# Later offsets for the side jobs that follow an attention in a four-layer attention and FFN kernel

## What is computed

```python
x = x + attn_a(layernorm(x))      # q, k, v, o projections, softmax over the past
x = x + ffn(layernorm(x))         # r = sigmoid(xr W_r); k = relu(xk W_k)^2; r * (k W_v)
x = x + attn_b(layernorm(x))      # k: decayed sum, normed, scaled; v: mixed with the next token's, normed
x = x + ffn(layernorm(x))
```

## Time and profile before

| | |
|---|---|
| median of 3 runs | 3308.53 us (3307.43 to 3314.87) |
| profiled execution, its own time | 3312.66 us |
| span of the trace in it | 3310.9 us |
| TensorE busy | 2950.6 us, 89% |
| ScalarE busy | 2226.6 us, 67% |
| VectorE busy | 1442.7 us, 44% |
| GpSimd busy | 830.9 us, 25% |
| mean granted TensorE clock | 0.944 of full speed |

### The profile page before, as it was taken

The page is one execution under the profiler, slowest core; times in us unless marked ns, Lnnn a source line. Parts: engine busy times, 40 slices in busy tenths (PEclk is TensorE's granted clock), DMA queues, the critical chain, the costliest instruction groups (busy, mean ns, idle before and its releaser), DMA issues.

```text
span 3310.9 us, 99622 instructions
## 1 busy us (share of the span) xinstructions
PE 2950.6 (89%) x42980; PEld 1307.6 (39%) x42980; DVE 1442.7 (44%) x3534; ACT 2226.6 (67%) x2487; POOL 830.9 (25%) x1278
## 2 busy tenths in 40 slices
PE   7799999999998799997998999998999988999887
PEld 3333343333434244443444444433333333333343
DVE  5232245545544652434333333444555545522444
ACT  2588876777776377673776677776777764777562
POOL 4122223233322222221222221322333321312111
PEclk9899999999999799997999999999999998999898
DMA  5222212222221123222222223221222221222111
GB/s 139 82 81 74 85 43 71 71 70 71 70 59 46 53 61 95 69 61 66 82 65 67 84 76 90 61 63 50 71 71 69 71 55 34 70 66 79 44 44 49
DMA packets 229841, 225.66 MB, mean 68 GB/s; under 512 B 33221, under 2 KB 212933, under 8 KB 229320
## 3 DMA queue, kind: packets, MB, share of 16 engines
q1 hardware_dynamic: 228504, 217.47, 23.0%
q10 hardware_dynamic: 816, 0.79, 0.1%
HBM read 146.80 MB, written 71.32 MB: 66 GB/s over the span
## 4 chain that ended last, share of the span: by engine, by line
PE 68%; DVE 17%; issue 8%; ACT 5%; POOL 1%; SPq 1%; DMA 1%; DVEq 0%; ACTq 0%; POOLq 0%
PE ps L857 42%; PE ps L1064 22%; ACT probs L813 4%; PE ps L869 3%; DVE pmax L1366 2%; DVE ln_st L1138 2%; DVE xn L1147 2%; DVE nw_u L1128 1%; DVE nw_u L1130 1%; DVE nw_y L1132 1%; DVE k_blk L1345 1%; DVE x_buf L1259 1%; DVE ln_mv L1141 1%; DVE o_blk L1408 1%; POOL probs L716 1%
## 5 line engine op out<-in xcount | busy, mean ns | idle before, releaser
L813 ACT ACTIVATE probs<-ps 128x1024 f32<-128x1024 f32 x2176 | 2078.0, 1093 | 714.5 <-PE ps L857 711.2
L857 PE MATMUL ps<-q_st,k_st 99*32 99x512 bf16 (+3 forms) x20480 | 1275.1, 353 | 43.2 <-issue 26.1
L1064 PE MATMUL ps<-probs,v_st 128*17 128x512 f32 (+3 forms) x10240 | 1201.0, 541 | 111.3 <-issue 76.5
L857 PEld LDWEIGHTS ps<-q_st,k_st 99*32 99x32 bf16 x20480 | 565.7, 97 | 850.8 <-issue 460.2
L716 POOL TENSOR_SCALAR_AFFINE_SELECT probs<-probs 128x256 f32<-128x256 f32 (+1 forms) x896 | 405.3, 468 | 1533.3 <-ACT probs L813 1526.5
L1064 PEld LDWEIGHTS ps<-probs,v_st 128*17 128x17 f32 x10240 | 288.7, 99 | 390.3 <-issue 169.5
L1408 DVE STREAM_TRANSPOSE o_blk<-ps 128x512 f32<-128x512 f32 x128 | 90.7, 709 | 449.6 <-PE ps L1064 447.7
L857 PE MATMUL ps<-xT,wT 128*32 128x512 f32 x2048 | 251.5, 609 | 1.8 <-issue 1.8
L869 PE MATMUL ps<-ident,xn 128*128 128x128 f32 x512 | 97.3, 323 | 117.6 <-DVE o_blk L1408 59.2
L1259 DVE TENSOR_TENSOR x_buf<-x_buf,ps 128x512 f32<-128x512 f32 x64 | 43.7, 683 | 316.9 <-PE ps L857 313.1
L640 POOL TENSOR_TENSOR parts<-rest,parts 128x512 bf16<-128x512 f32 x96 | 119.7, 1247 | 226.1 <-DVE parts L1170 226.1
(11 more groups left out here) (136 smaller groups left out, 2170.1 us busy)
## 6 DMA issues: line engine op xcount, KB each, us to landing
part_a<-parts SPq DMA_DIRECT2D x192, 128.0 KB
x_buf<-in_L_attn_a_X SPq DMA_DIRECT2D x32, 512.0 KB, 4.6
q_st<-part_a SPq DMA_DIRECT2D x128, 128.0 KB
o_chan<-o_out SPq DMA_DIRECT2D x64, 256.0 KB, 2.4
o_in<-o_chan SPq DMA_DIRECT2D x64, 256.0 KB, 4.5
q_st<-part_b SPq DMA_DIRECT2D x128, 128.0 KB
k_st<-part_a SPq DMA_DIRECT2D x64, 192.0 KB, 2.9
part_b<-parts SPq DMA_DIRECT2D x96, 128.0 KB
```

The lines of the kernel that those rows point to most:

```text
L813: nc.scalar.activation(probs[:, g % NP_BUF, :], ps[:, bk:bk + 2, :].rearrange("p a n -> p (a n)"), ACT.Exp, scale=SCALE[ATT[g // (NHG * NG ...
L857: last = pe.matmul(o[c:c + 32], kt[:, c:c + 32], q, **how)
L1064: last = pe.matmul(ps[32 * j:32 * j + VW, bank, q0:q0 + w], v_st[:, k % 2, kb, hg * HG + j, :], p, start=(kb == 0), stop=(kb >= TB * qc), ...
```

## The change

No instruction of the computation is added or removed; tables of offsets change, and with them the places at which parts stand. In the FFN half (`T_M`) the turns, `diff` and `shift` move back by 4 slots, `k0`, `k1`, `r0`, `r1` too, and `f0`, `f1`, `out` by 3. In the B half (`T_B`) `bt0` to `bv1` move back by 6 slots, `w` and `u` by 5, `vt0`, `vt1`, `len` and `split` by 4, `vb` by 2, `low` and `store` by 1; the layernorm before it (`lnb`) is numbered 3 later. The MB jobs of instances 28 to 31 keep the old offsets in a new table `T_END`; P jobs keep theirs. So that tables can differ from job to job, each job holds its own (`off`), and all steps read it there.

```diff
+    def __init__(self, kind, b, c, att, t0, off=None):
+        self.off = off or OFFSETS[kind]
...
-T_M = {"load": -10, "o0": 0, "o1": 2, "t0": 9, "t1": 11, "diff": 11, "shift": 13, "k0": 16, "k1": 18, "r0": 20,
-       "r1": 22, "f0": 25, "f1": 27, "out": 30}
-T_B = {"bt0": 34, "bt1": 36, "bk0": 38, "bk1": 40, "bv0": 42, "bv1": 44, "w": 46, "u": 48, "vt0": 51, "vt1": 53,
-       "len": 56, "split": 58, "vb": 64, "low": 67, "store": 71}
+T_M = {"load": -10, "o0": 0, "o1": 2, "t0": 13, "t1": 15, "diff": 15, "shift": 17, "k0": 20, "k1": 22, "r0": 24,
+       "r1": 26, "f0": 28, "f1": 30, "out": 33}
+T_B = {"bt0": 40, "bt1": 42, "bk0": 44, "bk1": 46, "bv0": 48, "bv1": 50, "w": 51, "u": 53, "vt0": 55, "vt1": 57,
+       "len": 60, "split": 62, "vb": 66, "low": 68, "store": 72}
+T_END = {"load": -10, "o0": 0, "o1": 2, "t0": 9, "t1": 11, "diff": 11, "shift": 13, "k0": 16, "k1": 18, "r0": 20,
+         "r1": 22, "f0": 25, "f1": 27, "out": 30}
...
-    jobs += [Job("MB", 2, c, 7, start(7, c) + FRONT if c < 3 else start(7, 2) + 32) for c in range(NCH)]
+    jobs += [Job("MB", 2, c, 7, start(7, c) + FRONT if c < 3 else start(7, 2) + 32, T_END) for c in range(NCH)]
...
-                  for name, off in {"P": (("ln", 0),), "MA": (("ln", 2), ("lnb", 27)), "MB": (("ln", 2),)}[j.kind])
+                  for name, off in {"P": (("ln", 0),), "MA": (("ln", 2), ("lnb", 30)), "MB": (("ln", 2),)}[j.kind])
...
-                yield j.t0 + T_M["diff"]
+                yield j.t0 + j.off["diff"]
```

More of the change, by code:

```diff
@@ L139, in job_list @@
             jobs.append(Job("P", b + 2, c, k + 1, start(k, c) + 29))
-    jobs += [Job("MB", 2, c, 7, start(7, c) + FRONT if c < 3 else start(7, 2) + 32) for c in range(NCH)]
-    jobs += [Job("MB", 3, c, 7, start(7, 3) + (16, 37, 58, 82)[c]) for c in range(NCH)]
+    jobs += [Job("MB", 2, c, 7, start(7, c) + FRONT if c < 3 else start(7, 2) + 32, T_END) for c in range(NCH)]
+    jobs += [Job("MB", 3, c, 7, start(7, 3) + (16, 37, 58, 82)[c], T_END) for c in range(NCH)]
     jobs.sort(key=lambda j: j.t0)
@@ L176, in number_parts @@
 def number_parts():
-    order = sorted((j.t0 + OFFSETS[j.kind][name], i, seq, name)
+    order = sorted((j.t0 + j.off[name], i, seq, name)
                    for i, j in enumerate(JOBS) for seq, name in enumerate(PE_PARTS[j.kind])
@@ L440, in m_job @@
             def m_job(j):
-                yield j.t0 + T_M["load"]
+                yield j.t0 + j.off["load"]
                 load_x(j)
                 load_o(j)
-                yield j.t0 + T_M["out"]
+                yield j.t0 + j.off["out"]
                 n = j.at["job"]
@@ L546, in _ @@
                     j = JOB["P" if ATT[k][0] == "A" else "MA", ATT[k][1], c]
-                    there = FIRST_SLOT if hg else j.t0 + (T_P["u3"] + T_P["store"] if j.kind == "P" else T_B["store"] + 2) + 2
+                    there = FIRST_SLOT if hg else j.t0 + (j.off["u3"] + j.off["store"] if j.kind == "P" else j.off["store"] + 2) + 2
                     loads.setdefault(max(free[0], there), []).append((load_queries, n, c))
@@ L644, in p_job @@
                 if j.c == 0:
-                    yield j.t0 + T_P["u0"]
+                    yield j.t0 + j.off["u0"]
                     if j.att >= 2:
@@ L700, in m_job @@
                 for m in range(KT):
-                    yield j.t0 + T_B["low"] + 2 * m
+                    yield j.t0 + j.off["low"] + 2 * m
                     low_part(j.at["unit"] + m)
@@ L914, in p_job @@
                         last.then_inc(s_part, 1)
-                if at == T_P["flag"] and j.c == NCH - 1:
+                if at == j.off["flag"] and j.c == NCH - 1:
                     part = j.at["flag"]
@@ L924, in m_job @@
                 for i in range(2):
-                    if at == T_M[f"o{i}"]:
+                    if at == j.off[f"o{i}"]:
                         if f == 0:
@@ L1263, in m_job @@
                 for kt in range(KT):
-                    yield j.t0 + T_M[f"t{kt}"]
+                    yield j.t0 + j.off[f"t{kt}"]
                     copy_out(j.at[f"t{kt}"], xf[:, kt, 1:CH + 1])
-                yield j.t0 + T_M["shift"]
+                yield j.t0 + j.off["shift"]
                 for buf, w, done in ((buf_k, 1, s_xk), (buf_a, 0, s_xr)):
@@ L1346, in m_job @@
                 settle()
-                yield j.t0 + T_B["split"]
+                yield j.t0 + j.off["split"]
                 for m in range(KT):
```

75 lines of the change are left out of this document (37 added, 38 removed).

## The result

| | before | after |
|---|---|---|
| median | 3310.93 us (4 runs beside those of after) | 3283.76 us (3280.78 to 3284.98) |
| ratio | 1 | 0.9916, 95% interval 0.9899 to 0.9933 |
| profiled execution's own time | 3312.66 us | 3280.78 us |
| span of its trace | 3310.9 us | 3279.1 us |
| mean granted clock | 0.944 | 0.958 |

The change makes the kernel faster by 27 us in the medians and by 31.8 us in the profiled executions, by their spans. Forecast were 44 us, a median of 3265 us, with 3225 to 3302 us as the range.

A forecast was written before the change was run, and what follows sets the result against it. TensorE, busy 89% of the span, sets the pace; its 360 us idle and lower-clock time can change. Terms -132 + 19 - 25 + 20 + 46 + 21 + 7 = -44 us gave 3265 us, range 3225 to 3302.

The forecast's parts named there:

- First turns, -132: Slots 5 to 12, 24 jobs: 8.6 us instead of 14.1, one 1.9 us wait left in slot 6; -132 us.
- Clock behind slot 6, +7: 24 jobs: a clock fall after the 1.9 us wait in slot 6, taken as 0.3 us a job; +7 us.
- the rival in which every job loses by it, and half of the gain with it: Slot 6's wait lowers the clock in every job; 53 us come back instead of 7; about 3310 us; chance 0.11.
- Masks behind `diff`, +19: Slot 14, 24 jobs: products wait 0.8 us for a GpSimd mask, bounds 0 and 1.5; +19 us.
- The rival that had the masks hidden: Clock stays up and masks are hidden, so +19, +21, +7 fall away; -91 us, 3218 us; chance 0.12.
- `bt0`, -25: Slot 30, 16 MA jobs: `bt0`'s 1.57 us wait for the layernorm goes; -25 us.
- slot 40, +20: 16 MA jobs: with `bt1` in slot 38, segment 3's first products wait 0.89 or 1.61 us; +20 us.
- End of an MA job, +46: 16 MA job ends: VectorE finishes later and `o1` starts 2.9 us later, bounds 2.2 and 3.5; +46 us.
- its clock, +21: 16 MA job ends: lower clock after TensorE's idle time makes `o1` cost 1.3 us more; +21 us.
- The clock rule that spoke against the change: A loop where TensorE waits each round is throttled each time; at `o1` every end pays 1.7 us, 27 instead of 21.
- All else, 0: Parts moved as blocks, the shorter `bv1` to `vt0` gap, SP loads and stores, ScalarE's exponentials: counted at nothing.

The follow-up runs named there:

- take_first: diff_apart with VectorE's layernorm behind `o1` placed behind the take of segment 3 instead of ahead of it; 3236.43 us, 0.9772.
- diff_apart: The changed kernel with the second token difference on GpSimd two slots behind the first; 3266.72 us, 0.9867.
- bt_early: The changed kernel with `bt0` and `bt1` alone two slots earlier, in slots 34 and 36; 3266.75 us, 0.9858.
- keys_apart: shift_two with key and value parts in turn (`bv0` in slot 38, `bk1` in 40, `bv1` in 42); 3189.68 us, 0.9642.
- shift_two: Against the kernel before: FFN-half steps and `bt0` to `bk0` two slots later, `bk1` one, everything from `bv0` on as before; 3212.27 us, 0.9700.
- low_behind: combo with `low` at 74 and `store` at 78, behind the masks of the next instance's first groups; 3236.57 us, 0.9767.
- combo: keys_apart with the split at 69, `vb` 66, `low` 70, `store` 74; 3215.48 us, 0.9713.

## Why the prediction was right, and where it was off

- **First turns, -132.** Right in mechanism: no wait ahead of the turns, one wait in slot 6, its releaser the take in 22 of 24 jobs. The stretch takes 9.05 us in MA jobs against 8.6 worked out, so 5.0 a job instead of 5.5. It counted the wait as the 1.9 us of a take that can't come earlier; take_first shows that it can.
- **Clock behind slot 6, +7.** Three stretches at clock 0.84 to 0.85 (instances 4, 19, 20) take 6 us more than the usual 8.9 in all, of which about 5 are the clock and the rest the longer wait. The size is right, and the rival in which every job loses by it, and half of the gain with it, is refuted. But this was luck. The forecast had a wait of 1.9 us and took the clock to stay up behind it; the wait came out at 1.1 to 1.7 us in twenty jobs. Over all fourteen kernels, where slot 6 held the only wait of its stretch, the clock fell behind 14 of 16 waits of 1.92 to 2.15 us. With a wait of the length forecast in every job, the rival could well have come true.
- **Masks behind `diff`, +19.** This is the term that was mis-sized: +39.6, 1.65 a job, over my upper bound of 1.5. The step that failed is the single wait of 0.8 us in slot 14. I let GpSimd catch up behind it. It does not: three of its six masks take 0.85 us beside VectorE's mixing, not 0.41, and to a wait of 0.49 us in slot 14 comes a second of 0.87 in slot 16. (The two make 1.36 us; the stretch grows by some 0.14 more for each, in diff_apart too.) At 0.41 us each the masks would be out 1.3 us earlier, which is more than 0.87, so by this estimate the second wait is the price of the overlap. The rival that had the masks hidden is refuted.
- **`bt0`, -25, and slot 40, +20.** -24.8 and +23.1. The waits of turns for a layernorm went from 54.0 us in 19 to 29.9 in 3; bt_early removes the wait of slot 40 alone.
- **End of an MA job, +46, and its clock, +21.** Over the twelve ends of instances 4 to 9 and 20 to 25 `o1` starts on average 2.87 us later than before (forecast 2.9) and takes 3.31 instead of 2.03 us, 1.28 more (forecast 1.3). Still the sixteen ends cost 59.9 us and not 67. Twelve (all but those of instances 8, 9, 10 and 26) cost 4.1 to 5.9, 57 us in all and 4.8 each where 4.2 were forecast: `o1` starts 3.0 us later there, takes 1.5 more, and 0.3 lie behind it. Instances 8 and 9, where `o1` was late before as well, cost 1.5 and 2.4, and 10 and 26, where slot 64 alone takes some 40 us, nothing. I had multiplied by 16 what holds for 12.
- **The clock rule that spoke against the change.** At `o1` the traces agree with the Trainium skill ("TensorE: Matmul & The Clock Gate", section "HAM oscillation — how this bites in real kernels"): eleven of the first twelve ends have an `o1` of 3.1 us or more, against 1.91 at the higher level. In slot 6, where TensorE also waits for data in every job, they don't: 1.00 in 21 of 24 stretches. The loop on that page waits longer, though, some 3 to 5 us.
- **All else, 0.** It is -8.9 us, of which -4 lie in slots 54 to 63 of MA jobs and some -4 at ends of instances without an MA job; I tested neither.

The sum is nearer than its terms. The turns, masks and slot 40 came out 28 us worse than forecast, the ends and all else 16 us better, and these cancel in part by luck.

What stays open: no run moved VectorE's mixing away from the masks. That they stretch by it rests on the comparison of masks with and without it in the same trace.

## What to carry to other kernels

When side work is moved later in an interleaved order, move it no further than the wait needs: two slots back (71 us under after) took the wait at the turns and left the last engine's work where it was. Ask of every bank what stands ahead of its release in the releasing engine's own order; here one `yield` that puts a take ahead of a layernorm was worth 30 us, and putting 5 us of work ahead of a release lost 26. When a wait for several semaphores names one releaser, check its time against all others: the mask named in slot 1 had ended 1.0 us before, and the kernel built on it was to gain 15 us or more over keys_apart and lost 47. Before a step of GpSimd is moved, look at what VectorE runs in its new place: `low` beside the layernorm cost more than `low` beside the split.

## What the runs showed of the hardware

- The granted clock of slots 5 to 11, where slot 6 held the only wait over 0.15 us from slot 67 on, over the traces of all fourteen kernels: behind 37 waits of 0.92 to 1.53 us it stayed at 1.00 each time, behind 68 of 1.70 to 1.73 it fell once (shift_two, instance 23, 0.84), behind 16 of 1.92 to 2.15 it fell 14 times, to 0.84 or 0.85, and behind 6 of 3.13 to 4.09, all in low_behind, each time. Behind the wait of 3.89 us ahead of `o1` it was 0.50, and `o1` took 3.81 us against 1.91.
- On GpSimd a mask of 128 x 256 takes 0.40 to 0.41 us with VectorE idle (348 in after) and 0.85 to 0.86 where it runs beside VectorE's step of line 1273 with two SBUF inputs (49 in after); one of 128 x 512 takes 0.63 us and 1.08 (diff_apart). Beside a transpose or the layernorm's statistics, with one input, it stays at 0.40 to 0.42; beside the layernorm's scaling `xn<-x_buf`, which reads one tile too, it takes up to 0.55.
- On VectorE the subtraction `rest` takes 0.69 us, and 1.53 us where GpSimd's `low` runs beside it (combo; low_behind has 0.69 in the same place). The layernorm's small steps on 128 x 4, integer ones (lines 1124, 1126) and others (1129, 1131, 1133, 1144), take some 0.9 to 1.1 us where they run into `low`; the two integer steps take 0.17 us each without it.
- The Trainium skill ("GPSIMD Engine Reference", section "Specifications") says that GpSimd shares its SBUF interfaces with VectorE, and that VectorE's steps with two SBUF inputs or in a 2-port mode contend for them. The masks beside line 1273 and the two times of `rest` agree for steps with two inputs. The slowed integer steps and `xn` read one tile; which mode they ran in no trace here shows.
